# One state-space block on one core: each part stored once, copies made memory to memory, and two casts moved to ScalarE

## The reference, cut to what matters

```
xz = xn @ W_in;  xi, z = split(xz)
u = silu(causal_conv(xi, 4 taps) + conv_b)
dt_r, B, C = split(u @ W_xproj)
delta = softplus(dt_r @ W_dt + b_dt)
A = -exp(A_log)
h[t] = h[t-1] * exp(delta[t] * A) + (delta[t] * u[t]) * B[t]
y[t] = sum over states of h[t] * C[t]
out = x + ((y + u * D) * silu(z)) @ W_out
```

## Time and profile before

| | us |
|---|---|
| median of 3 runs | 5863.85 (5862.06 to 5864.1) |
| profiled execution | 5866.2 |
| its span | 5864.4 |
| VectorE busy | 5532.8 (94%) |
| TensorE busy | 5246.8 (89%) |
| ScalarE busy | 3525.5 (60%) |
| GpSimd busy | 2302.3 (39%) |

### The profile page before, as it was taken

The page is one execution under the profiler, slowest core; times in us unless marked ns, Lnnn a source line. Parts: engine busy times, 40 slices in busy tenths (PEclk is TensorE's granted clock), DMA queues, the critical chain, the costliest instruction groups (busy, mean ns, idle before and its releaser), DMA issues. The chain is left out here.

```text
span 5864.4 us, 150087 instructions
## 1 busy us (share of the span) xinstructions
PE 5246.8 (89%) x38780; PEld 2480.8 (42%) x38780; DVE 5532.8 (94%) x3683; ACT 3525.5 (60%) x8302; POOL 2302.3 (39%) x6767
## 2 busy tenths in 40 slices
PE   2999959999999999999999999999999999997999
PEld 1444324444444444444444444444444444445666
DVE  5799989999999999999999999999999999995776
ACT  6777746666666666666666666666666666662333
POOL 4000024444454444444444444444444444440111
PEclk7999979999999999999999999999999999998999
DMA  4899962222222222222222222222222222224342
GB/s 156 298 334 334 340 197 53 53 54 55 55 52 53 54 55 55 52 54 54 55 54 51 55 54 55 54 52 54 55 54 53 52 54 55 54 45 142 118 137 74
DMA packets 1105510, 547.19 MB, mean 93 GB/s; under 512 B 753744, under 2 KB 1015056, under 8 KB 1105056
## 3 DMA queue, kind: packets, MB, share of 16 engines
q1 hardware_dynamic: 1093776, 533.89, 33.8%
q10 hardware_dynamic: 11664, 12.52, 0.6%
HBM read 296.83 MB, written 249.82 MB: 93 GB/s over the span
## 5 line engine op out<-in xcount | busy, mean ns | idle before, releaser
L988 DVE TENSOR_TENSOR_SCAN s_h<-s_decay,s_ubank 128x1024 f32<-128x1024 f32 x2048 | 4461.0, 2261 | 13.5 <-ACT s_ubank L953 13.3
L940 ACT ACTIVATE s_decay<-s_abank 128x512 f32<-128x512 f32 x4096 | 2210.3, 595 | 2.2 <-PE s_abank L878 1.1
L863 PE MATMUL s_ybank<-s_h,s_window 128*8 128x256 f32 x16416 | 1948.3, 602 | 1.9 <-DVE s_h L988 1.9
L904 PE MATMUL s_ubank<-s_x,s_w 128*128 128x256 bf16 x8192 | 1246.3, 275 | 371.2 <-DVE s_h L988 370.8
L1024 POOL TENSOR_TENSOR s_carry<-s_decay,s_h 128x64 f32<-128x64 f32 x2032 | 884.2, 435 | 1750.4 <-ACT s_decay L940 1577.2
L953 ACT ACTIVATE s_ubank<-s_seed 128x64 f32<-128x64 f32 x2048 | 478.2, 233 | 1710.3 <-PE s_ubank L904 1326.8
L878 PE MATMUL s_abank<-xnT,s_a 128*128 128x256 bf16 x8192 | 1257.0, 274 | 33.0 <-DMA s_w<-scratch_b_rows 29.9
L904 PEld LDWEIGHTS s_ubank<-s_x,s_w 128*128 128x128 bf16 x8192 | 675.8, 98 | 1193.4 <-DVE s_h L988 1091.7
L878 PEld LDWEIGHTS s_abank<-xnT,s_a 128*128 128x128 bf16 x8192 | 758.4, 98 | 197.7 <-ACT s_decay L940 40.2
L863 PEld LDWEIGHTS s_ybank<-s_h,s_window 128*8 128x8 f32 x16416 | 377.9, 97 | 838.8 <-issue 729.8
L1028 POOL TENSOR_TENSOR s_seed<-s_carry,s_first 128x64 f32<-128x64 f32 x2048 | 660.2, 322 | 164.3 <-ACT s_first L946 3.9
(11 more groups left out here) (129 smaller groups left out, 3194.1 us busy)
## 6 DMA issues: line engine op xcount, KB each, us to landing
s_x<-scratch_u_rows SPq DMA_DIRECT2D x4096, 32.0 KB
scratch_u_rows<-p_u_turn SPq DMA_DIRECT2D x90, 1024.0 KB, 6.7
scratch_delta_rows<-p_dparts SPq DMA_DIRECT2D x136, 512.0 KB, 6.2
xnT<-scratch_delta_rows SPq DMA_DIRECT2D x1024, 64.0 KB, 2.7
scratch_y<-s_y SPq DMA_DIRECT2D x1036, 16.0 KB
scratch_sz<-p_sz SPq DMA_DIRECT2D x16, 1024.0 KB, 6.2
scratch_u<-p_u SPq DMA_DIRECT2D x16, 1024.0 KB, 7.9
s_w<-scratch_b_rows SPq DMA_DIRECT2D x256, 64.0 KB, 2.4
```

Of the source, the lines that this page charges most:

```text
L863: last = nc.tensor.matmul(y_bank[32 * ct:32 * ct + WIN, 1 - x, :], window[:, of, (at + t) * WIN:(at + t + 1) * WIN], H[:, 1 - x, :, t], st ...
L904: last = nc.tensor.matmul(dst.rearrange("p q (a t) -> p a q t", t=2), w2[:, g, 4 * s + 2 * x + e, :], x2[:, s, :, 2 * x + e, q:q + 32, :], ...
L940: nc.scalar.activation(dst.rearrange("p x q t -> p q x t"), a_bank[:, b].rearrange("p j r (x t) -> p (j r) x t", x=2), ACT.Exp).then_inc(e ...
L988: nc.vector.tensor_tensor_scan(H[:, x, PT * p:PT * p + PT, :].rearrange("p q t -> p (q t)"), decay[:, x * (1 + c % 2), p].rearrange("p q t ...
```

## The change

COPIES becomes one store per part. In the project stage back_stores stores three delta places and turn_stores three u places. The remaining five delta places and two u places of each tile are filled by copy_rows: a transfer from device memory to device memory, issued by SP, 0.52 MB for a delta place and 1.05 MB for a u place. The seven copies of tile 0 are issued in the project stage, after tile 12; those of tile i + 1 in the scan stage, one behind each even chunk of tile i (seven of its eight), and the scan waits for them at the start of a tile.

The second part of delta and of delta*u is made by ScalarE (second_delta, second_u) around Abs; VectorE makes the third part of delta after the rest of delta*u, and the third part of delta*u after B's parts (split_last).

```diff
-COPIES = (2, 2, 1, 1)
+COPIES = (1, 1, 1, 1)
...
             def back_stores(i, c, b):
+                sp.wait_ge(d2_done, i + 1)
                 sp.wait_ge(d3_done, i + 1)
-                for k, (_, j) in reversed(list(enumerate(COMBOS))):
+                for k, (_, j) in reversed(list(enumerate(COMBOS[:3]))):
                     sp.dma_start(tile_of(d["delta_rows"][k], i), dparts[:, j]).then_inc(dparts_stored, 16)
...
-                        if j == part and k < PLACES:
+                        if j == part and k < 3:
...
                 back_stores(i, c, b)
+                if isinstance(b, int) and c == 0:
+                    sp.wait_ge(dparts_stored, 16 * 3 * (i - 1))
+                    for j in range(3):
+                        sp.wait_ge(turns_stored[j], 16 * COPIES[j] * (i - 1))
+                    for n in range(N_COPIES):
+                        copy_rows(sp, d, 0, n, copied)
...
+            def second_delta(i):
+                act.wait_ge(dr_done, i + 1)
+                nc.scalar.activation(dparts[:, 1], w1[:, :, :], ACT.Identity).then_inc(d2_done, 1)
+
+            def second_u(i):
+                act.wait_ge(ur_done, i + 1)
+                nc.scalar.activation(uparts[:, 1], du[:, :, :], ACT.Identity).then_inc(u2_done, 1)
...
+                second_delta(i)
                 act.wait_ge(back_read, i * 7 + 12)
                 nc.scalar.activation(ex[:, :, :], v[:, :, :], ACT.Abs).then_inc(abs_done, 1)
+                second_u(i)
...
+            act.wait_ge(cleared, 4)
...
+            nc.vector.memset(w1[:, :, :], 0.0).then_inc(dr_done, 1)
+            nc.vector.memset(du[:, :, :], 0.0).then_inc(ur_done, 1)
...
+                dve.wait_ge(delta_done, i + 2)
+                dve.wait_ge(dparts_stored, i * 48 + 48)
+                nc.vector.tensor_copy(dparts[:, 0], lw[:, :, :]).then_inc(d1_done, 1)
+                dve.wait_ge(d1_done, i + 1)
+                nc.vector.tensor_tensor(w1[:, :, :], lw[:, :, :], dparts[:, 0], ALU.subtract).then_inc(dr_done, 1)
+                dve.wait_ge(du_done, i + 3)
+                dve.wait_ge(turned, i * 8 + 16)
+                nc.vector.tensor_copy(uparts[:, 0], du[:, :, :]).then_inc(u1_done, 1)
+                dve.wait_ge(u1_done, i + 1)
+                nc.vector.tensor_tensor(du[:, :, :], du[:, :, :], uparts[:, 0], ALU.subtract).then_inc(ur_done, 1)
+                dve.wait_ge(d2_done, i + 2)
+                nc.vector.tensor_tensor(dparts[:, 2], w1[:, :, :], dparts[:, 1], ALU.subtract).then_inc(d3_done, 1)
...
+            def split_last(i):
+                dve.wait_ge(u2_done, i + 3)
+                nc.vector.tensor_tensor(uparts[:, 2], du[:, :, :], uparts[:, 1], ALU.subtract).then_inc(u3_done, 1)
...
+def copy_rows(eng, d, i, n, done):
+
+    if n < NCB - 3:
+        cols = bass.ds(i * TW + TW, TW)
+        eng.dma_start(d["delta_rows"][3 + n][:, cols], d["delta_rows"][n % 3][:, cols]).then_inc(done, 16)
+    else:
+        k = n - (NCB - 3)
+        rows = bass.ds(i * TW + 2 * TW, TW)
+        eng.dma_start(d["u_rows"][rows, 3 + k, :], d["u_rows"][rows, k, :]).then_inc(done, 16)
...
+            def tile(i, more):
+                sp.wait_ge(copied, i * (16 * N_COPIES) + 16 * N_COPIES)
+                for k in range(per):
+                    chunk(i * (per // 4) + k // 4, i * per + k, k % 4)
+                    if more and k % 2 == 0 and k // 2 < N_COPIES:
+                        copy_rows(sp, d, i + 1, k // 2, copied)
```

More of the change, by code:

```diff
@@ L402, in project_stage @@
         turns_stored = [sem(f"turns_stored{j}") for j in range(4)]
+        copied = sem("p_copied")
         n_weights = 10
@@ L481, in _ @@
             sp.wait_ge(sz_stored, 16 * (NT + 1))
-            sp.wait_ge(dparts_stored, 16 * NCB * (NT + 1))
+            sp.wait_ge(dparts_stored, 16 * 3 * (NT + 1))
             sp.wait_ge(c_stored, 16 * (NT + 1))
@@ L485, in _ @@
                 sp.wait_ge(turns_stored[j], 16 * COPIES[j] * (NT + 3))
+            sp.wait_ge(copied, 16 * N_COPIES)
         @block.tensor
@@ L518, in turn @@
                 if g == 0:
+                    pe.wait_ge(u2_done, i + 1)
                     pe.wait_ge(u3_done, i + 1)
@@ L557, in _ @@
             act.sem_inc(turn_read, 11)
+            act.sem_inc(u2_done, 1)
             act.wait_ge(weights, 16 * n_weights)
@@ L630, in _ @@
                     take_turn(i, g)
+                if i == NT:
+                    second_delta(NT)
+                    second_u(NT)
         @block.vector
@@ L713, in step @@
                 split_b(i)
+                split_last(i)
             front(0, 0, 0)
@@ L731, in _ @@
                                     pattern=[[-1, P]], channel_multiplier=1).then_inc(ident_ready, 1)
+N_COPIES = NCB - 3 + PLACES - 3
+def copy_rows(eng, d, i, n, done):
[6 more added lines that the diff above has]
+        eng.dma_start(d["u_rows"][rows, 3 + k, :], d["u_rows"][rows, k, :]).then_inc(done, 16)
 def scan_stage(nc, d, xnT):
@@ L778, in scan_stage @@
         y_stored = [sem("y_stored0"), sem("y_stored1")]
+        copied = sem("s_copied")
         block = ctx.enter_context(nc.Block())
@@ L798, in _ @@
             sp.dma_start(a_w[:, :, :, :].rearrange("p f j m -> p (f j m)"), d["a_image"]).then_inc(a_loaded, 16)
+            sp.sem_inc(copied, 16 * N_COPIES)
             deltas = d["delta_rows"].rearrange("c (h f j r) t -> r (c h) f j t", h=2, f=HALVES, r=ROWS)
@@ L837, in chunk @@
                 store_y(f, c % 2, f * 2 + 1)
-            over_chunks(sp, chunk)
+            per = NF // NT
+            def tile(i, more):
[4 more added lines that the diff above has]
+                        copy_rows(sp, d, i + 1, k // 2, copied)
+            with sp.Fori(0, NT - 1) as i:
+                tile(i, True)
+            tile(NT - 1, False)
             for f in range(NF, NF + 3):
```

## The result

| | before | after |
|---|---|---|
| median of 5 runs, us | 5863.01 (5862.06 to 5864.1) | 5895.65 (5894.89 to 5895.72) |
| ratio | | 1.0055, 95% interval 1.004 to 1.007 |
| span of the profiled execution, us | 5864.4 | 5893.9 |

The changed kernel is 32.6 us slower, outside the range of 5847 to 5880 us. The page first: the rows that answer to the earlier trace rows, and the instruction queue's row.

The account below looks back on a forecast made before the run. VectorE was taken to bound both stages. Casts +9.2, last chain -2.5, drain -9.1 and copies 0 summed to -2.4 us, subtracted from the median 5863.85 for 5861.4 us; range 5847 to 5880 us.

Parts of the forecast that it names:

- The 105 copies: Scan stage: SP's copies behind even chunks' y stores are covered and gone before the s_x loads; 0 us.
- up to 6 us: Scan stage: the time taken for one copy to hold the DMA engines, between bounds of 2.7 and 11.4 us.
- rival C: Scan stage: copies make s_x late; one us late costs some +65 us, giving 5927 us; chance 0.08.
- The two casts: Project stage: two casts add 3.64 us a tile to ScalarE, 58.2 us against 49.0 us of room; +9.2 us.
- the last chain: Project stage's end, after the last Exp: VectorE's last chain gets its two casts back; -2.5 us.
- The drain: Project stage's end: with fewer stores the DMA engines drain sooner, so the scan stage starts sooner; -9.1 us.
- The first tile's copies: Last batch of the project stage: seven copies delay only a store asked for a tile later; nothing, else 8 us once.
- A: Project stage: VectorE keeps what the casts save, 40 us and the drain's 9.1, giving 5815 us; chance 0.06.
- B: Freed DMA engines shorten other things, such as loop-turn intervals, by sooner instruction fetches; 3 to 12 us; chance 0.08.
- D: Project stage: ScalarE's chain grows more than its casts through p_v gaps, 27 us at worst; 5875 us; chance 0.10.
- the prediction's lower bound of 2.7 us: Scan stage: the least time a 1.05 MB copy holds the DMA engines, at 385 GB/s.

Follow-up runs that it names:

- experiment 5: The changed kernel with only SP's scan loop written out, its casts, single stores and all copies kept: 5852.52 us (0.9984).
- experiment 11: Against the kernel before: single stores and the copies, both casts still on VectorE, SP's scan loop written out: 5850.77 us (0.9979).
- experiment 4: The changed kernel with SP's scan loop at 4 chunks a turn, a tile's copies regrouped in quarters, three transfers a turn: 6042.6 us (1.0307).
- experiment 12: Against the kernel before: single stores, copies, SP's scan loop written out, only delta's second part cast on ScalarE, delta*u's on VectorE: 5832.52 us (0.9947).
- experiment 3: The kernel before, without copies, with SP's scan loop written out as 256 chunks: 5860.41 us (0.9996).

## Why the prediction was wrong, point by point

**The 105 copies, "Sum: 0": here it failed.** The copies themselves are as predicted. An issue takes 0.65 us, and their page rows after give a landing of 4.1 us for 0.52 MB and of 5.4 us for 1.05 MB, within the "up to 6 us" that I took:

```profile
scratch_delta_rows<-scratch_delta_rows SPq DMA_DIRECT2D x80, 512.0 KB, 4.1
scratch_u_rows<-scratch_u_rows SPq DMA_DIRECT2D x32, 1024.0 KB, 5.4
```

But the step counted issues and transfers alone and never read the last lines of the diff as a change of the loop: one body of 16 chunks (about 1,300 instructions) took the place of one of four (322). Each of its 14 jumps then holds SP for 3.1 to 3.4 us in place of 0.4. The step also looked only at the odd chunks, whose loads stand behind a copy. A jump stands ahead of delta's loads and so ahead of an even chunk's s_x loads (1075.82 above), which by the prediction's own words "have no time to spare". The lost time is 38.6 us in the trace, 43 us by experiment 5, some 2 of them for the faster issue of the written-out loop. The sign the prediction named for rival C (s_firstbank waits for a DMA) did appear, with another cause: the loads were late because SP was, 2 us once a tile, and C's 65 us or more would have come from every odd chunk.

The Trainium skill has the rule that I should have weighed: Advanced Engine Details and Errata, section "ISA Cache", gives an engine other than TensorE 32 KB for instructions, in two lines of 256 instructions. By it 1,300 instructions of 64 bytes, 83 KB, can't stay loaded over a turn, and the trace agrees (12 transfers a jump). On the line the runs differ, and decide: a transfer is 8.2 KB, 128 instructions, and with two lines of 256, wherever their borders lie, the loops at 335 to 668 and at 438 to 759 can't both be refetched while the one at 429 to 750 is kept. All nine loops of four chunks (seven positions) fit three neighbouring blocks of 128 instructions with a border between 751 and 759, a place that I fitted to the runs: within three, nothing is fetched (429 to 750, 557 to 878 twice, 399 to 732, 675 to 997); where a fourth is touched, each jump brings five transfers (438 to 759 twice, 335 to 668; and by its stalls 739 to 1061). The longer bodies fit too: with these borders they touch 6 blocks (429 to 1070) and 11 (429 to 1710, and 334 to 1631 in the changed kernel), and each jump brings 7 and 12 transfers, one more than the blocks in every case. That a fourth block of the Trainium skill's 32 KB is taken by reading ahead would fit, and wasn't tried.

**The two casts, +9.2, and the last chain, -2.5: right in kind, too dear by 6 us.** Each added 1.80 us to ScalarE, 0.02 below the price taken: from the first cast to the table load behind Abs and the second it is 744.24 - 738.72 = 5.52 us in the timeline after, where Abs alone took 452.39 - 450.47 = 1.92 before. From the first L693 to the last it is 542.0 us; before, 542.1. With the last chain's -2.8 us and the first tile's +3.3, the end of the memset moved by +0.5 us where +6.7 was forecast. VectorE's wait came out as said in size (39.0 us in 15 waits) but not in place: it stands at the third part of delta, for the first cast, and not at L693 for Exp. So ScalarE's chain had room beyond the 49.0 us of waits for L666. Part of it was at p_xi, where its waits for TensorE fell by 4.6 us; at p_v they rose by 2.8 us, and the rest isn't located. ScalarE's waits at 200 to 800 us, before and after:

```profile
ACT p_v L592 <- PE p_bk L511: 37.7, 56, 1.3
...
ACT p_xi L567 <- PE p_in L494: 14.0, 21, 1.4
```

```profile
ACT p_v L611 <- PE p_bk L520: 40.5, 56, 1.3
ACT p_xi L578 <- PE p_in L503: 9.4, 15, 1.6
```

The equal sum hides a spread. Before, the intervals with a convolution were 36.6 us but for three of 37.0 to 37.7. After, they follow ScalarE's waits at p_v: 35.5 us where these are 1.9 us in a tile, 37.4 us where they are 3.7, and 39.6 at one turn of the program's loop. With the loop well placed the pair changes nothing that can be told: 5866.38 against 5865.23 us, and 5852.52 against 5850.77.

**The drain, -9.1: right.** -9.0 us (0.4 us behind the memset in place of 9.4), and -9.1 of the -9.6 us of experiment 11.

**The first tile's copies, 0: right.** Fourteen intervals with a convolution sum to 719.01 - 205.45 = 513.6 us after and 515.2 before. (The fifteenth, without one, grew from 26.9 to 28.5 us.)

**The rivals.** A is refuted for two casts, though five intervals are below 36 us, and true in kind for one. B: the store's landings fell (delta's 6.2 to 4.0 us, u's 6.7 to 4.2) and nobody waited for them. It has the remark that instructions are fetched: I thought of that as a gain, not of what triggers a fetch. D: its mechanism is there, for ScalarE's waits at p_v now lengthen a tile and the interval of 39.6 us holds a gap of 1.02 us at p_v. But they grew by 2.8 us in all, not by up to 27, and no loss came of it.

Without the jumps the sum was -9.7 us (5852.52 against 5862.21), some 2 of them from the written-out loop; with them +32.6.

## What to carry to other kernels

When a diff rewrites a loop on an engine that issues transfers, count its body's instructions and where it begins, and look at the instruction queue's row first: transfers that grow with the number of turns mean that each jump is paid, here 2.5 to 3.2 us. An edit far away that shifts such a loop by a few instructions can cost more (here 3%) than the edit is about, so an ablation that misses by a constant per turn should be checked for this before its own mechanism is blamed. And work moved to another engine pays up to the room in its chain and no further: one cast of 1.8 us against 3.3 us of room gave 18 us, two gave nothing.

## What the runs showed of the hardware

- SP's loop of 322 instructions has a gap of 0.7 us at its jump where it lies well, and of 3.0 to 3.3 us where it lies 9 instructions later; over 63 jumps +176 us of 5863.
- The loss is per jump, hardly by length: 2.5 and 2.6 us with bodies of 8 and 16 chunks, 2.8 us with 4 chunks (176 us in 63 jumps), 3.0 us in experiment 4 (180 us in 59).
- Written out, SP issues 16 loads in 5.67 us in place of 7.25 us and four stores in 1.32 us in place of 1.70 us (SP's timelines of experiment 12 and of the changed kernel). In SP's timeline of experiment 12:

```profile
3017.64 5.89 SPq L875 DMA_DIRECT2D s_x<-scratch_u_rows  x16
3023.63 1.31 SPq L854 DMA_DIRECT2D scratch_y<-s_y  x4
...
3036.44 5.67 SPq L875 DMA_DIRECT2D s_x<-scratch_u_rows  x16
```

- Written out, the instructions are fetched too, without stalls: 98 transfers in the whole kernel of experiment 3, and no gap above 0.2 us between y's stores and delta's loads. Reading straight on is hidden here; a jump back to a body that has to be fetched is not.
- A copy of 1.05 MB within device memory filled the DMA engines for two to three us and then left them, as the prediction's lower bound of 2.7 us had it; the four windows add up to 1.01 MB, so its bytes are counted once. Windows of 1 us after the changed kernel's issue at 978.34, with the DMA share and GB/s as the last columns:

```profile
980.00:981.00 1.00, 1.00 (x13) 0.36 (x14) 1.00 (x1) 1.00 (x5) 0.81 (x3) 1.00 0.79 199
981.00:982.00 1.00, 1.00 (x14) 0.13 (x4) 1.00 (x2) 0.69 (x2) 0.39 (x1) 1.00 1.06 395
982.00:983.00 1.00, 1.00 (x11) 0.70 (x8) 1.00 (x1) 0.03 (x1) 0.62 (x3) 1.00 1.00 391
983.00:984.00 1.00, 0.52 (x6) 0.22 (x5) 1.00 (x2) 1.00 (x3) 0.00 (x0) 1.00 0.08 27
```
